# One 512-column multiplication in place of four subtract-and-scale instructions in the first layer norm of a GNN kernel

## What is computed

```python
# layer 0: an edge network and a maximum over the edges of each dst
feat = concat([x[dst], x[src] - x[dst]]); h = relu(feat @ W1 + b1)
x = layernorm(x + segment_max(h @ W2 + b2, dst))        # 0 for rows without an edge
# layer 1: a sum over the edges of each dst, two products and a residual product
h = x + segment_sum(x[src], dst)
x = layernorm(x + x @ Wres + bres + relu(h @ w1 + b1) @ w2 + b2)
```

## Time and profile before

| | |
|---|---|
| median of three runs | 1114.36 us |
| the profiled execution | 1113.68 us, span 1111.9 us |
| PE busy | 1068.9 us, 96% |
| DVE busy | 934.9 us, 84% |
| ACT busy | 896.9 us, 81% |
| POOL busy | 765.8 us, 69% |
| x1 (L609) | 784 instructions, 221.7 us, 361 ns each |
| granted TensorE clock, mean | 0.995 |

### The profile page before, as it was taken

How to read it: one execution, slowest core, us unless ns; L and a number is a source line. 1 busy time by engine, 2 the same in 40 slices (tenths; PEclk the granted TensorE clock), 3 DMA queues, 4 the chain that set the end, 5 groups by cost and what they waited for, 6 DMA issues and landing times.

```text
span 1111.9 us, 27074 instructions
## 1 busy us (share of the span) xinstructions
PE 1068.9 (96%) x7463; PEld 835.6 (75%) x7463; DVE 934.9 (84%) x3645; ACT 896.9 (81%) x3888; POOL 765.8 (69%) x798
## 2 busy tenths in 40 slices
PE   5899999999999999999899999999999999999995
PEld 3677877777666666666578888888888878888884
DVE  7799888897888888888868787878787789999993
ACT  2887878787888888888897888888888887777774
POOL 6777777777777777772047777777777777777712
PEclk9999999999999999999999999999999999999998
DMA  5788877875888888877576667676756566666652
GB/s 151 214 244 247 230 244 231 246 233 152 220 222 232 248 232 221 233 223 214 164 232 198 213 191 215 190 214 191 214 166 194 172 202 217 218 217 220 218 171 86
DMA packets 172255, 231.86 MB, mean 209 GB/s; under 512 B 25658, under 2 KB 90791, under 8 KB 172106
## 3 DMA queue, kind: packets, MB, share of 16 engines
q1 hardware_dynamic: 145434, 180.66, 52.0%
q0 software_dynamic: 25088, 48.94, 17.3%
q10 hardware_dynamic: 1584, 0.53, 0.2%
HBM read 129.48 MB, written 102.78 MB: 209 GB/s over the span
## 4 chain that ended last, share of the span: by engine, by line
PE 65%; POOL 19%; issue 8%; DVE 4%; ACT 2%; DMA 1%; SPq 0%; POOLq 0%; DVEq 0%; ACTq 0%
POOL edge_rows L522 17%; PE psY L1125 10%; PE psY L1126 10%; PE psH L1137 10%; PE psE L1118 6%; PE psT L1118 5%; PE psE L1257 4%; PE psE L1126 4%; PE psE L1125 4%; PE psE L1293 4%; PE psE L1248 3%; PE psE L1242 3%; PE psE L1240 3%; POOL xd_early L522 1%; DVE shared L758 1%
## 5 line engine op out<-in xcount | busy, mean ns | idle before, releaser
L1125 PE MATMUL psY<-wc,hT 128*128 128x128 f32 x1568 | 304.1, 276 | 0.5 <-DVE o_rows L646 0.4
L1126 PE MATMUL psY<-wcr,xT 128*128 128x128 f32 x1568 | 303.9, 276 | 0.0
L522 POOL DMA_INDIRECT edge_rows<-x1e_table,idx x196 | 188.8, 963 | 118.5 <-issue 59.4
L526 POOL DMA_INDIRECT out<-edge_rows,idx x196 | 195.0, 995 | 100.0 <-issue 61.9
L1125 PEld LDWEIGHTS psY<-wc,hT 128*128 128x128 f32 x1568 | 240.7, 192 | 13.3 <-issue 13.3
L949 ACT ACTIVATE junk<-psY 128x128 f32<-128x128 f32 x784 | 209.3, 302 | 49.3 <-PE psY L1126 49.1
L1126 PEld LDWEIGHTS psY<-wcr,xT 128*128 128x128 f32 x1568 | 238.8, 193 | 0.0
L522 POOL DMA_INDIRECT edge_rows<-in_x,idx x196 | 189.8, 968 | 65.5 <-issue 59.4
L609 DVE TENSOR_SCALAR x<-x_in,mv,rs 128x128 f32<-128x128 f32 x784 | 221.7, 361 | 0.6
L1137 PE MATMUL psH<-xT,wc 128*128 128x512 f32 x392 | 204.5, 604 | 6.2 <-ACT xT L944 5.5
L1118 PEld LDWEIGHTS psT<-ident,x 128*128 128x128 f32 x784 | 99.2, 143 | 110.1 <-issue 104.1
(11 more groups left out here) (125 smaller groups left out, 1993.4 us busy)
## 6 DMA issues: line engine op xcount, KB each, us to landing
x_in<-in_x SPq DMA_DIRECT2D x196, 256.0 KB
out<-o_rows SPq DMA_DIRECT2D x195, 256.0 KB
src_bc<-src_dram SPq DMA_DIRECT2D x49, 256.0 KB, 4.5
mask<-mask_dram SPq DMA_DIRECT2D x98, 128.0 KB
x1eT_spill<-x1eT SPq DMA_DIRECT2D x49, 256.0 KB, 2.4
x1e_table<-edge_rows SPq DMA_DIRECT2D x49, 256.0 KB, 3.5
x1e_table<-shared SPq DMA_DIRECT2D x49, 256.0 KB, 3.8
x1eT<-x1eT_spill SPq DMA_DIRECT2D x49, 256.0 KB, 3.1
```

The costliest lines, as they stand in the source:

```text
L522: nc.gpsimd.indirect_dma_start(to, None, table, bass.IndirectOffsetOnAxis(idx[:, what, t:t + 1], 0)).then_inc(landed[n % FLIGHT], 16)
L526: nc.gpsimd.indirect_dma_start(table, bass.IndirectOffsetOnAxis(idx[:, SCAT, t:t + 1], 0), frm, None, bounds_check=limit, oob_is_err=False ...
L1125: t_.matmul(to[:, cut(t)], h[:, cut(t)], wc2[:, :], start=t == 0, stop=False, skip_group_check=True)
L1126: last = t_.matmul(to[:, cut(t)], xt[:, cut(t)], wcr[:, :], start=False, stop=t == TILES - 1, skip_group_check=True)
```

## The change

`norm1_scale` no longer calls `center_scale`, which goes. In place of four TENSOR_SCALAR of 128x128, each with two numbers per row (the mean and `rs`), there is one TENSOR_TENSOR of 128x512 that multiplies `x_in` with `rs` alone, broadcast along each tile. The mean is not subtracted. Waits, buffers and semaphores are those of before; `bn_aggr` is kept, since the variance comes from it.

```diff
-            def center_scale(to, rows, mv, rs, done):
-
-                for t in range(TILES):
-                    last = v.tensor_scalar(to[:, cut(t)], rows[:, cut(t)], mv[:, t, 0:1], rs[:, t:t + 1],
-                                           ALU.subtract, ALU.mult)
-                last.then_inc(done, 1)
-
...
                     slot = (n - 2) % SLOTS
                     dve.wait_ge(rstd_done, n + 1)
                     wait(dve, t_done, n - 1)
-                    center_scale(x1[:, n % 2, :], x_in[:, n % SLOTS, :], mv[:, slot, A_ROWS, :], rs[:, slot, A_ROWS],
-                                 x1_done)
+                    v.tensor_tensor(tiles(x1[:, n % 2, :]), tiles(x_in[:, n % SLOTS, :]),
+                                    rs[:, slot, A_ROWS].unsqueeze(2).broadcast_to([P, TILES, P]),
+                                    ALU.mult).then_inc(x1_done, 1)
```

## The result

| | before | after |
|---|---|---|
| median | 1114.92 us (4 runs, 1113.69 to 1116.23) | 1128.85 us (4 runs, 1128.13 to 1129.63) |
| span of the profiled execution | 1111.9 us | 1127.8 us |
| DVE busy | 934.9 us | 849.1 us |
| x1 | 784 instructions, 221.7 us | 196 instructions, 133.8 us |

The ratio is 1.0128, with a 95% interval of 1.0112 to 1.0143: 14 us slower, where 4.4 us faster was forecast. A few executions took 9% longer or more than the others of the same kernel, and the medians here leave them out. The first thing to read is the page of the changed kernel, its busy times and two of its rows over the span, in which one slice is new. Each digit is the busy share of 1/40 of the span (28 us), in tenths.

What follows compares the result with a forecast made beforehand. PE was taken to bound the kernel, at 96% of the span. Ten phase A loops (4.2 us) and the loop before them (0.18 us) sum to 4.4 us: 1114.36 - 4.4 = 1110.0 us, eight-in-ten range 1107.8 to 1112.8.

Steps and rivals of the forecast that it cites:

- The price of the new instruction: One 128x512 TENSOR_TENSOR on DVE takes 0.61 us to the next start, against 1.03 us for four TENSOR_SCALAR: 0.42 us less.
- Phase A: Ten loops, 300 to 545 us, where PE's center_z waits for DVE: each 0.42 us shorter, 4.2 us in all.
- Before 293 us: nothing: Head and phase S gain nothing: PE waits for POOL's unbroken row of gathers, which no x1 stands in front of.
- rival B: 62 multiplications before 290 us each hold up one gather by 0.39 us: 24 us later, 1134 us; chance 0.04.
- The head: Opening stretch, where PE waits for DVE and ACT: up to 1.7 us if uncovered, costed at nothing.
- Rivals A and C: A: another wait takes over in phase A, 1111.6 to 1114.4 us, chance 0.14; C: gathers get faster, 1107.8 us, chance 0.05.

Runs made afterwards that it cites:

- only_a: Kernel before the change, with the new multiplication only for the units of phase A and the four behind it (61 to 76): 1109.83 us beside 1114.83, ratio 0.9953.

## Why the prediction was wrong

**The price of the new instruction: right.** 682 ns median; in the loop of phase A the reciprocal starts 313.15 - 312.55 = 0.60 us behind x1, against 0.61 worked out.

```profile
312.55 0.68 DVE L629 TENSOR_TENSOR x<-x_in,rs 128x512 f32<-128x512 f32 x1
313.15 0.19 DVE L732 RECIPROCAL rs_e<-sd_e 128x8 f32<-128x8 f32 x1
```

**Phase A: right.** The waits of L1251 fell from 0.73 to 0.31 us (0.32 forecast), and the units come 339.18 - 316.10 = 23.1 us apart, against 23.5 before. Between 316.10 and the last loop at 547.03 the lag on the kernel before falls from 19.4 to 15.2 us, by 4.2 (531.85 was its place there). Phase C stayed at 3.09 us per unit. only_a measured the forecast by itself: 1109.8 against 1110.0.

```profile
547.03 1.16 PE L1251 MATMUL psE<-center,shared 128*128 128x128 f32 x8 [0.31 <-DVE shared L763]
```

**"Before 293 us: nothing": the step that failed.** It rested on one sentence, that no x1 stands in front of the row of gathers, "so it ends when it ends". That holds for waits on semaphores. But the engines also meet where no semaphore shows it, and 45 held gathers in 62 units, about 0.3 us a unit (19.2 us in all), moved the end of the row from 279.1 to 297.7 us. I had seen that PE was only just supplied at 292.88 us; with a slack of nothing, every microsecond of delay counted in full.

**The dismissal of rival B: the reading that was wrong.** The mechanism, its place, the count of 62 and the point where it decides (0.07 us each) were all on paper; its chance was set to 0.04. The reason given was a mean: 0.948 us per gather in phase B, where L808 has two SBUF inputs, against 0.951 in phase S. A mean cannot show this. In phase B a step takes 6.17 us and five gathers take 5 x 1.25 = 6.25 us. So the row moves against L808 by only about 0.1 us a step, and meets it in about one step of eight. Where it does meet it, the gather is plain in the trace of before:

```profile
585.60 0.69 DVE L808 TENSOR_TENSOR xsT<-shared,x1eT 128x512 f32<-128x512 f32 x1
...
585.81 1.30 POOL L522 DMA_INDIRECT edge_rows<-x1e_table,idx  x1 [0.30 <-issue]
```

The 1.33 us gather that I quoted in the earlier trace rows was a question that I did not ask: what was DVE doing there? It started at 284.08 us, 0.23 us behind L769, which has two SBUF inputs:

```profile
283.85 0.75 DVE L769 SCALAR_TENSOR_TENSOR shared<-shared,bias_cols,xdT 128x512 f32<-128x512 f32 x1
```

The 754 ns of L808 that served as upper bound came from such a meeting too, one in which DVE was the one delayed. And phase S did have held gathers, a 1.15 us one among every ten, by L667. The sentence "the rows show neither" about the Trainium skill's rule was false; that both kinds of instruction hold a gather was already in the trace.

**The price of rival B: near, in part by luck.** 0.39 us in each of 62 units, 24 us, 1134 us. It was 0.44 to 0.45 us, but in 45 units: 19 us more in the row, 20.7 us of waiting, and 1128.85 us. A price too low and a count too high partly made up for each other. The head gave back more than I had priced: PE came to group 4 4.2 us earlier and not 1.7. I did not follow where it gained them beyond the first 60 us, in which it is busy for 45.6 us instead of 42.7.

**Rivals A and C** did not occur. For C there is this much: L609 held 24 gathers and scatters by 0.09 us, 2 us in all.

The sum from the rows: +17.7 us when PE is through group 4, +2.1 from the low clock (19.8), -0.4 by the loop that follows (19.4), -4.2 in the ten loops (15.2), and 15.9 at the end of the span. The last 0.7 us was not followed up.

## What to carry to other kernels

A busy DVE that is off PE's path may still hold up GpSimd: before four short instructions are joined into one long one with both inputs in SBUF, look at what GpSimd does meanwhile and how much slack its chain has. Test such a rule by pairs in time, each gather with the DVE instruction that it starts under, and not by the mean duration of a stage, which depends on how the two periods fall together. And where a row of transfers is issued in one unbroken chain, put first what is wanted first: here a new order of the gathers, with x1 one line up in phase A, turned 14 us of loss into 10 us of gain while the multiplications held as many gathers as before.

## What was not expected of the hardware

- A gather is held by some of the DVE instructions that it starts under, and let go at a fixed time from the instruction's start: 0.45 us by 128x512 with two SBUF inputs, 0.22 us by a one-input 128x512 of 478 ns, 0.11 us by 128x128 pieces with two inputs, though four of these follow each other without a gap. Nothing by 0.69 us instructions with one input in PSUM.
- A held gather sets the whole row to DVE's period: 40 of 47 multiplications met a gather at the same distance, 0.11 to 0.14 us. A row of 1.25 us steps beside a period of 4.25 us does not drift over it by chance.
- DVE itself hardly waited: x1's multiplication took 657 to 712 ns in all 196 cases, and the 712 ns were those of one that started 0.01 us behind a gather. L808 and its successor L802 took up to 0.07 us longer than their 693 ns in such meetings.
- After 18 us without work PE's granted clock was at the 1.2 GHz level. It stayed there from 300 to 304 us (0.50), where PE was busy for 1.39 us between waits for single gathers, and for 4 to 5 us of work after it (0.53 from 304 to 309 us), where 2.1 us were lost.
